# GpSimd takes two weighings of each attention group, block numbers are loaded a group ahead, and the mixture copies its turned weights before mixing

## The reference, cut to what matters

```
x = x + attention(layernorm(x))      # q.k per edge and head, softmax over a node's incoming edges, sum of a*v
x = x + top1_experts(layernorm(x))
x = x + relational(layernorm(x))     # scores from h_all[edge_type, src] and h_all[edge_type, dst], softmax, sum of w*h_src
x = x + top2_experts(layernorm(x))

attn = einsum('ehd,ehd->eh', k[src], q[dst]) + attn_bias
a = exp(attn - segment_max(attn, dst)[dst]);  a = a / segment_sum(a, dst)[dst]
out = segment_sum(v[src] * a[:, :, None], dst)
```

## Time and profile before

| | us |
|---|---|
| median of three runs | 5146.75 |
| lowest, highest | 5141.87, 5160.14 |
| the profiled execution | 5098.82 |
| its span, first to last instruction | 5097.0 |
| busy in it: PE, DVE, ACT, POOL | 4158.7, 3118.0, 1833.6, 2199.5 |

### The profile page before, as it was taken

How to read it: one execution, slowest core, us unless ns; L and a number is a source line. 1 busy time by engine, 2 the same in 40 slices (tenths; PEclk the granted TensorE clock), 3 DMA queues, 4 the chain that set the end, 5 groups by cost and what they waited for, 6 DMA issues and landing times. The chain is left out here.

```text
span 5097.0 us, 80743 instructions
## 1 busy us (share of the span) xinstructions
PE 4158.7 (82%) x21797; PEld 3128.1 (61%) x21798; DVE 3118.0 (61%) x8508; ACT 1833.6 (36%) x5242; POOL 2199.5 (43%) x2307
## 2 busy tenths in 40 slices
PE   8587777777778991999899587777877769999998
PEld 4355555555557991999544265555555548788887
DVE  5399999999995441111222177677777765555554
ACT  2254544454442330333233244444444412222222
POOL 5456766666652333000222366666666621111111
PEclk9799999999999995999999777887778879999999
DMA  6556666666642115111344333333333320000000
GB/s 195 173 153 173 183 180 176 179 181 182 174 142 105 39 42 211 34 37 37 115 179 178 132 92 99 99 100 99 98 100 99 98 72 14 14 14 14 14 15 11
DMA packets 231099, 542.47 MB, mean 106 GB/s; under 512 B 46073, under 2 KB 128525, under 8 KB 221998
## 3 DMA queue, kind: packets, MB, share of 16 engines
q0 software_dynamic: 112976, 348.83, 24.6%
q1 hardware_dynamic: 117854, 190.49, 10.7%
HBM read 423.60 MB, written 115.55 MB: 106 GB/s over the span
## 5 line engine op out<-in xcount | busy, mean ns | idle before, releaser
L269 POOL DMA_INDIRECT attn_KV<-kv_tab,attn_stage x832 | 881.3, 1059 | 447.8 <-issue 252.4
L1789 POOL DMA_INDIRECT rel_V<-h_tab,rel_stage x832 | 849.4, 1021 | 451.7 <-issue 226.1
L1888 PE MATMUL rel_SP<-rel_V,rel_OH 128*128 128x264 f32 x1664 | 638.2, 506 | 172.1 <-DVE node L1958 132.5
L382 PE MATMUL attn_SP<-attn_KV 128*128 128x264 f32 x1664 | 559.1, 425 | 243.9 <-DVE node L483 177.3
L382 PEld LDWEIGHTS attn_SP<-attn_KV 128*128 128x128 f32 x1664 | 270.4, 191 | 480.6 <-issue 240.8
L1888 PEld LDWEIGHTS rel_SP<-rel_V,rel_OH 128*128 128x128 f32 x1664 | 342.3, 238 | 324.1 <-DVE node L1958 190.8
L370 PE MATMUL attn_QP<-node,attn_OHT 128*128 x1664 | 458.7, 401 | 52.9 <-issue 32.3
L2167 ACT ACTIVATE moe_HT<-moe_HB,moe_b 128x128 f32<-128x128 f32 x800 | 228.6, 368 | 669.4 <-PE moe_HB L2183 669.4
L1958 DVE TENSOR_TENSOR node<-node,rel_SP 128x264 f32 x832 | 348.5, 419 | 185.3 <-remote 87.8
L2183 PE MATMUL moe_HB<-moe_YT,moe_W 128*128 128x128 f32 x3200 | 410.9, 283 | 0.0
L483 DVE SCALAR_TENSOR_TENSOR node<-node,same,attn_SP 128x264 f32 x832 | 393.2, 473 | 25.9 <-PE attn_SP L382 14.6
(11 more groups left out here) (331 smaller groups left out, 6989.7 us busy)
## 6 DMA issues: line engine op xcount, KB each, us to landing
h_tab<-pr_H SPq DMA_DIRECT2D x50, 1056.0 KB
attn_KV<-kv_tab,attn_stage POOLq DMA_INDIRECT x832
rel_V<-h_tab,rel_stage POOLq DMA_INDIRECT x832
kv_tab<-qkv_KV SPq DMA_DIRECT2D x50, 256.0 KB
attn_runs<-runs SPq DMA_DIRECT2D x52, 192.0 KB
rel_runs<-runs SPq DMA_DIRECT2D x52, 192.0 KB
Wd<-in_wd SPq DMA_DIRECT2D x8, 1024.0 KB
y_sorted<-gate_zeros SPq DMA_DIRECT2D x8, 928.0 KB
```

Of the source, the lines that this page charges most:

```text
L269: pool.indirect_dma_start(out=KV[:, i * IT + u, 0:2 * FEAT], out_offset=None, in_=d["kv_tab"][:, :], in_offset=bass.IndirectOffsetOnAxis(a ...
L382: pe.matmul(SP[u % SUMS][:, 0:NUMC], KV[:, j * IT + u, 0:P], KV[:, j * IT + u, FEAT:ROW], start=True, stop=True).then_inc(s["sums"], 1)
L1789: pool.indirect_dma_start(out=V[:, i * IT + u, :], out_offset=None, in_=d["h_tab"][:, :], in_offset=bass.IndirectOffsetOnAxis(ap=stage[:, ...
L1888: pe.matmul(SP[(j + u) % SUMS][:, 0:NUMC], OH[:, j * IT + u, :], V[:, j * IT + u, :], start=True, stop=True).then_inc(s["sums"], 1)
```

## The change

Four things. In attention GpSimd weighs pairs 6 and 7 of group k - 3 between its gathers for group k, ahead of the fifth and the ninth, with a semaphore of its own (`pool_weighted`) that TensorE's `sum_pair` waits for; VectorE weighs pairs 0 to 5 (`OWN`). After the last gather GpSimd weighs these pairs of the last three groups. In attention and in the relational stage both engines load the block numbers one group ahead, at another place of the period, and keep two sets of registers. In the mixture the copy of the turned weights stands ahead of the mixing of pair 0.

```diff
@@ attention, GpSimd
+                def weigh(c, j, v):
+                    if has(c, G):
+                        pool.wait_ge(s["w_copied"], c + 1)
+                        at = j * IT + 2 * v
+                        rows = KV[:, at:at + 2, FEAT:2 * FEAT].rearrange("p s (a b) -> p s a b", b=DH)
+                        pool.tensor_tensor(rows, rows, KV[:, at:at + 2, 2 * FEAT:ROW].unsqueeze(3).to_broadcast([P, 2, HEADS, DH]),
+                                           ALU.mult).then_inc(s["pool_weighted"], 1)
...
                                 need(pool, s["sums"], (k - RING) * IT + (u + 2))
+                            if u == 4 or u == 8:
+                                weigh(k - RING, i, OWN + u // 4 - 1)
...
                 every_period(pool, body, PERIODS)
+                for c in range(G - RING, G):
+                    for v in range(OWN, PAIRS):
+                        weigh(c, c % RING, v)
@@ attention, TensorE
-                        pe.wait_ge(s["weighted"], c * PAIRS + (v + 1))
+                        if v < OWN:
+                            pe.wait_ge(s["weighted"], c * OWN + (v + 1))
+                        else:
+                            pe.wait_ge(s["pool_weighted"], c * (PAIRS - OWN) + (v - OWN + 1))
...
-                    to = blocks_of(k, mybir.EngineType.PE) if has(k, G) else None
+                    to = ahead_of.get(k)
...
                     dst_rows(k, i, to, 7)
+                    if has(k + 1, G):
+                        ahead_of[k + 1] = blocks_of(k + 1, mybir.EngineType.PE)
                     sum_pair(c, n, 6)
@@ attention, VectorE
-                    if has(c, G) and v < PAIRS:
+                    if has(c, G) and v < OWN:
...
-                    blks = blocks_of(c, mybir.EngineType.DVE) if has(c, G) else None
+                    blks = ahead_of.get(c)
...
                             factor(g)
+                        if v == 7 and has(c + 1, G):
+                            ahead_of[c + 1] = blocks_of(c + 1, mybir.EngineType.DVE)
                         add(c, blks, 2 * v)
@@ relational, TensorE
-                    packed = blocks_of(k, mybir.EngineType.PE) if has(k, G) else None
+                    packed = ahead_of.get(k)
                     dst_rows(k, packed, 0)
...
                     dst_rows(k, packed, 3)
+                    if has(k + 1, G):
+                        ahead_of[k + 1] = blocks_of(k + 1, mybir.EngineType.PE)
                     sum_pair(c, n, 5)
@@ relational, VectorE
-                    packed = blocks_of(c, mybir.EngineType.DVE) if has(c, G) else None
+                    packed = ahead_of.get(c)
                     rescale(c, packed)
...
                             dst_scores(k, 1)
+                            if has(c + 1, G):
+                                ahead_of[c + 1] = blocks_of(c + 1, mybir.EngineType.DVE)
...
                         add(c, n, packed, 2 * v + 1)
@@ mixture, VectorE
-                    mix_pair(t, i, 0)
                     if has(t, BLOCKS):
                         dve.wait_ge(s["c_turned"], t + 1)
                         dve.tensor_copy(CT[:, :], c_turned).then_inc(s["cT"], 1)
+                    mix_pair(t, i, 0)
```

More of the change, by code:

```diff
@@ L192, in attention_layer @@
     SUMS = 2
+    OWN = PAIRS - 2
     ROW = 2 * FEAT + HEADS
@@ L196, in attention_layer @@
         s = sems(nc, m, "attn", "staged far masks turned turned_sb q_rows product reduced st_turned biased scan rows row_sums rows_l "
-                 "cols most neg exp w_turned w_copied rows_f fac_in fac_out fac_less factor rescaled rescale weighted moved sums added "
+                 "cols most neg exp w_turned w_copied rows_f fac_in fac_out fac_less factor rescaled rescale weighted pool_weighted moved sums added "
                  "cleared")
@@ L430, in body @@
                         pe.matmul(pfac, KV[0:1, j * IT, 0:P], fac[0:1, 3, :], start=True, stop=True).then_inc(s["factor"], 1)
+                ahead_of = {0: blocks_of(0, mybir.EngineType.PE)}
                 for q in range(2):
@@ L542, in _ @@
                 dve.wait_ge(s["cleared"], 1)
+                ahead_of = {}
                 def body(k, i, turn):
```

## The result

The changed kernel takes 5109.19 us (5103.9 to 5110.24, five runs) against 5144.22 for the kernel before beside it: a ratio of 0.9925, interval 0.9909 to 0.994, 35 us. The forecast was 5001 with a range of 4905 to 5075, so it is wrong. Its profiled execution took 5108.1 us (span 5106.3), one under its median; that of the kernel before lay 45 under its own, so profile against profile the change is 9 us *slower*. It isn't known on which chip the profile of the kernel before was taken. So differences of stages between the two profiles hold for the mixture, whose blocks took the same time on every chip, and overstate what the change costs in attention.

A forecast was written before the change was run, and what follows sets the result against it. VectorE was taken to bound attention, TensorE the mixture, no engine the relational stage, with GpSimd bounding attention after the change. Gains of 30 + 36 + 79.5 = 145.5 us from 5146.75 gave 5001, range 4905 to 5075.

The forecast's parts named there:

- 21.9 - 0.4 + 2 x 1.45 = 24.4 us: Attention: GpSimd's work per group with two weighings and one gather hold less, taken as the new bound over VectorE's 23.14.
- the 0.67 pauses at the head: Attention: VectorE's waits for a group's first query rows, expected to go with the moved loads but counted as no gain.
- 30 us of gain: Attention: moving two weighings to GpSimd saves 0.63 us in each of 47 groups; bounds 81 gained to 27 lost.
- 1.45 forecast: Attention: us per GpSimd weighing, from two passes at 0.91, 0.39 for the step from gather, and half a pause.
- In attention "nothing": Moving the attention register loads gains nothing: VectorE's new place has 1.6 us queued against 1.10, TensorE's precedes a wait.
- 36 us were forecast: Relational stage: moved register loads save 0.96 - 0.25 = 0.71 us in each of 51 groups; bounds nothing to 83.
- rival (c): Relational stage: loads give nothing, as the 2 us wait after them is for TensorE's results and stays; 5037 us, chance 0.08.
- 79.5 forecast: Mixture: the earlier copy of turned weights removes TensorE's 49 waits of 1.62 us ahead of the router's logits.
- The upper bound that I had kept apart: Mixture: 20 us more if about 13 stretches at 1.2 GHz, 1.5 us each, go with the pause.
- (a): Attention: GpSimd's weighing is cheap, about 0.9 us, VectorE stays the bound near 23.5; gain 72, 4959 us, chance 0.20.
- (b): Attention: GpSimd's weighing is dear or holding works both ways; groups of 25.6, 27 us lost, 5058 us, chance 0.16.
- (d): Attention: strided, broadcast weighing takes over 3.2 us on GpSimd, groups of 27.9, attention loses 115 us or more; chance 0.04.

The follow-up runs named there:

- e11: Changed kernel with SyncE's five transfers of an attention group waiting for the second product of the group before: 4698.6 us, ratio 0.9708 to the kernel before.
- e16: Changed kernel with GpSimd filling each set of attention rows in place of gathering it: 4873.0 us, ratio 0.9477 to the kernel before, one run.
- e2: Kernel before with only TensorE's register load of the attention stage moved a group ahead: 5100.7 us, ratio 1.0004.
- e3: Kernel before with only VectorE's register load of the attention stage moved behind a group's last product: 5117.0 us, ratio 1.0042.
- e13: Kernel before with GpSimd's weighing, the mixture's edit and SyncE's five transfers a group moved, register loads in their old places: 4714.0 us, ratio 0.9743.
- e12: Kernel before with the mixture's edit and SyncE's five transfers a group moved, nothing else: 4738.0 us, ratio 0.979.
- e4: Kernel before with only the mixture's copy of the turned weights placed ahead of the mixing of pair 0: 4991.5 us, ratio 0.9785.
- the last six runs: Follow-ups on one chip where the kernel before took 5142 us; they include the changed kernel again, 5108.5 us, ratio 0.994.
- e1: Kernel before with only GpSimd's weighing of pairs 6 and 7; register loads and mixture as they were: 5164.4 us, ratio 1.0128.
- e18: Changed kernel with GpSimd issuing gather 14 of an attention group only behind the group's first product: 5045.3 us, ratio 0.9807.
- e15: Changed kernel with attention gathers of 1 KB a row in place of 2, same number of gathers: 5118.4 us, ratio 0.9955, one run.

## Why the prediction was wrong

**The bound in attention.** The sum took a group for the longest engine's own work. That engine was named wrongly even where nothing is held: GpSimd's work was put at 21.9 - 0.4 + 2 x 1.45 = 24.4 us with VectorE's 23.14 below it, and in e11 VectorE sets the group of 23.63, its 23.14 and the 0.44 for which GpSimd's weighing holds it, with GpSimd some 0.4 below. e16, with GpSimd idle more than half of the time, has 23.46. The step that failed by more is the one on the 0.67 pauses at the head, which "should go, but under a GpSimd bound they are worth nothing". They were the small end of the holds, and with the edit the head met the full one: 3.4 us in most of 41 pauses, 135.8 us. The forecast had 30 us of gain there; the runs have some 70 of loss (below). Why a hold is longer with the edit stays open; that gathers are needed for it is shown (e16). Two rows should have raised the doubt: the wait of 27.99 us beside the earlier trace rows, which I read past as the start of the stage, and the 2 us waits for TensorE in the relational stage whose end had nothing to do with when TensorE finished.

**Price of the weighing.** 1.45 forecast. Measured are 1.06 for the second of a group, which nothing of VectorE's holds, and 1.34 in the mean for the first (1.58 in e11), so 1.20 for the two in the changed kernel. The free one is nearest to the 1.12 estimated from the Trainium skill's GPSIMD Engine Reference (section 3.1).

**Register loads.** In attention "nothing": right for TensorE's (e2, 1.0004), wrong for VectorE's (e3, 1.0042, 17 to 22 us; why isn't shown, its head wait is 39.2 where e2 has 23.5). In relational 36 us were forecast; the 0.96 went and the group didn't shorten, 24.15 against 24.22 on one chip. That is rival (c), for its reason: the wait for TensorE takes the place. Without holds the group is 0.15 to 0.35 us shorter, some 8 to 18 us in all (e11 against e13 and e12).

**Mixture.** Mechanism right, size too small: 79.5 forecast, 105 between profiles, 108 in e4. The upper bound that I had kept apart, the stretches at 1.2 GHz that go with the pause, came in whole: between the first and the last block the profile of before has 13 of them, that of after none, and each made its block 1.67 longer: 22 us. The rest is in the undisturbed blocks, 15.22 and 16.57 in turn where they were 17.50 and 17.68: 1.7 a block and not 1.62, 83 us.

**Rivals.** (a) is what the chip without holds shows: VectorE the bound at about 23.5 (measured 23.63), though GpSimd's weighing is dearer than its 0.9. (b)'s holding works in both directions, as it said: the maximum's 0.34 became 0.72 beside a weighing of GpSimd's, 0.44 us a group or 21 us over the stage; VectorE's own weighings are mostly not the ones held (median 0.683 us where it was 0.673, the longest 1.80). (The Trainium skill, SBUF — State Buffer, "Who interferes with whom", calls the ports that the two share an exclusive lock, and the rows agree: of each pair one goes through at its usual length and the other waits it out, the maximum ending 0.16 behind the weighing at 1077.90, a first weighing of GpSimd's taking 1.66 in place of 1.06 beside VectorE's 0.68.) (d), the slower side, had the right sign for attention with a mechanism that didn't occur.

**The sum** as it came, between profiles: attention +105, mixture -105, relational +9, together +9. Between medians the change is 35 us faster, and medians of one chip are the fair comparison. With the mixture's 105 taken off, attention and the relational stage together cost 70 us there, and 72 on the chip of the last six runs (5108.5 against 5141.8). The relational groups being equal, nearly all of it is attention's, which fits e1's 65 for the weighing alone. That split is an estimate, as no profile of the kernel before exists for either chip.

**Better kernels.** On chips with holds e4 (0.9785) and e18 (0.9807), each on its own, lie together within their intervals, both ahead of the changed kernel (0.9925, 0.994). On the one without, the changed schedule (e11, 0.9708) beats the mixture alone (e12, 0.979) by 39 us, both with SyncE's transfers moved, and 0.64 x 47 = 30 of them are in attention. That is the forecast's own term, and its whole, 5001/5146.75 = 0.972, is near what e11 has. Both are luck: the bound was VectorE and not GpSimd, the relational stage gave at most half of its 36 us and the mixture 25 more than its 79.5. The mixture's copy is worth 105 us on every chip (blocks of 17.99 us in all eight profiles without it, 15.83 to 15.90 in all twelve with it; 108 by the medians of e4); the weighing pays only where nothing is held.

## What to carry to other kernels

A wait for an engine whose work is long done is not slack, and its length is not a constant: find what is running during it before counting an engine's own time as the bound. Beside gathers, moving anything by a microsecond cost more here than the edit saved, so test each edit alone. Look at every instruction of the engine that was relieved, as one that nobody counted grew by 0.38 us a group. And compare kernels, and profiles too, on the same chip: chips of the same kind were 6% apart here, and which edit wins changed with them.

## What the runs showed of the hardware

- While GpSimd issues gathers back to back (one in 1.25 us), TensorE's results reach ScalarE, VectorE and GpSimd late on most chips, and several at once: up to 4.1 us (the factor) and 5.1 us (the query rows shown) at the head of a group, 29 at the start of the stage. With no gathers the copy of the factor starts 0.88 or 0.89 us after its matmul in all of 47 groups (e16). With gathers of half the bytes: as with whole ones (e15, one run).
- Beside GpSimd's weighing a VectorE instruction that reads two operands from SBUF is held until the weighing is over (0.339 us to 0.722), and GpSimd's weighing is held by VectorE's in the same way (1.06 to 1.66).
- The late results depend on the chip. The kernel before took 4839 us on one and 5100 to 5152 on the others; on the first, no product of VectorE waited for its query rows in a group of the steady part.
- Where results are late, the profile also lacks half or more of the gathers' semaphore records (4159 of 9872 there, 11376 of 11376 in e11). What inside the chip holds the results is open, and so is whether the recording has a part in it. Not tried: an execution without recording, other ways to gather, and a gather of fewer rows.
